# Gated attention with routed experts on one core: token grouping in fewer steps, GpSimd takes mixes, masks and row numbers, four row buffers

## What is computed

```python
xn = _layernorm(x, axis=-1)
s = _L0_attn_ref(xn, ...)          # softmax(q k^T / 4) v, combined with lambda, layernorm, @ Wo + bo
h = jnp.mod(x_flat[:, :2].sum(axis=1).astype(jnp.int32), 8)      # x_flat = xn
sel = jnp.stack([h, jnp.mod(h + 1, 8)], axis=1)
w = jnp.any(sel == e, axis=1) / 2
y = jnp.maximum(x_flat @ W1e + b1e, 0.0) @ W2e + b2e             # for each expert e, acc + w * y
x = x + s * _silu(acc)
```

## Time and profile before

| | us |
|---|---|
| median of 3 runs | 412.05 |
| lowest, highest | 411.11, 412.3 |
| the profiled execution, its own time | 411.52 |
| its span in the profile | 409.6 |
| TensorE busy | 381.5 (93%) |
| VectorE busy | 291.8 (71%) |
| ScalarE busy | 267.5 (65%) |
| GpSimd busy | 189.3 (46%) |

### The profile page before, as it was taken

One profiled execution on the slowest core, in us unless ns is written; L12 is line 12 of the kernel. 1 busy time (PEld: TensorE's weight loads), 2 busy tenths in 40 slices (PEclk: granted clock), 3 DMA queues, 4 the chain that ended last, 5 costly groups with the idle time before them and its releaser, 6 DMA issues.

```text
span 409.6 us, 8427 instructions
## 1 busy us (share of the span) xinstructions
PE 381.5 (93%) x2576; PEld 248.3 (61%) x2576; DVE 291.8 (71%) x758; ACT 267.5 (65%) x667; POOL 189.3 (46%) x262
## 2 busy tenths in 40 slices
PE   4996989999999999999999999999999999999993
PEld 2353876565775667766665668765676667764321
DVE  7787996656686757766676767866686767866884
ACT  3581756666765776576666767676766668675783
POOL 7944203454456543565355532663573444541200
PEclk9996999999999999999999999999999999999999
DMA  7975953263216451265105640346136141216740
GB/s 263 343 230 112 242 196 91 80 206 105 79 37 191 111 195 21 79 190 168 46 27 170 189 140 18 136 121 197 48 127 216 22 169 47 81 26 213 230 159 26
DMA packets 36945, 54.75 MB, mean 134 GB/s; under 512 B 6724, under 2 KB 25141, under 8 KB 36903
## 3 DMA queue, kind: packets, MB, share of 16 engines
q1 hardware_dynamic: 31456, 46.94, 34.6%
q0 software_dynamic: 3296, 6.76, 7.8%
q10 hardware_dynamic: 2151, 0.53, 0.6%
HBM read 15.59 MB, written 6.75 MB: 55 GB/s over the span
## 4 chain that ended last, share of the span: by engine, by line
PE 74%; DVE 7%; DMA 5%; ACT 4%; SPq 4%; issue 4%; POOL 1%; ACTq 0%; DVEq 0%; POOLq 0%
PE ring L1393 14%; PE pv_bank L1327 13%; PE ring L1414 12%; PE score L1289 12%; PE exp L1314 10%; PE ring L1251 3%; DVE neg_max L1049 3%; DMA xs<-xn_rows,inverse 3%; SPq L532 2%; PE ring L1335 2%; PE ring L1255 1%; PE ring L1353 1%; PE ring L1276 1%; PE ring L1375 1%; PE score L1264 1%
## 5 line engine op out<-in xcount | busy, mean ns | idle before, releaser
L1049 DVE TENSOR_REDUCE neg_max<-score 128x1 f32<-128x512 f32 x256 | 169.0, 683 | 72.3 <-PE score L1289 66.7
L1289 PE MATMUL score<-ks,qs 96*128 96x512 bf16 x256 | 98.3, 386 | 6.3 <-DVE neg_max L1049 6.0
L787 ACT ACTIVATE probs<-exp 128x512 f32<-128x512 f32 x124 | 72.5, 605 | 36.3 <-PE exp L1314 32.3
L787 ACT ACTIVATE xin<-exp 128x512 f32<-128x512 f32 x120 | 69.7, 604 | 38.5 <-PE exp L1314 38.1
L1314 PE MATMUL exp<-qs,ks 99*128 99x512 bf16 x244 | 91.7, 380 | 0.1
L825 ACT ACTIVATE hT<-ring,pair 128x128 f32<-128x128 f32 x256 | 73.4, 377 | 13.0 <-PE ring L1393 11.9
L1414 PEld LDWEIGHTS ring<-w_sb,hT 128*128 128x128 f32 x568 | 73.5, 191 | 10.4 <-issue 3.5
L1414 PE MATMUL ring<-w_sb,hT 128*128 (+1 forms) x568 | 75.4, 275 | 0.9 <-ACT hT L825 0.9
L1393 PEld LDWEIGHTS ring<-xsT,pair 128*128 128x128 f32 x512 | 66.3, 191 | 14.6 <-issue 8.1
L1393 PE MATMUL ring<-xsT,pair 128*128 128x128 f32 x512 | 68.2, 276 | 1.7 <-issue 1.2
L684 POOL TENSOR_SCALAR tanh<-tanh 128x128 f32<-128x128 f32 x32 | 17.2, 536 | 95.5 <-ACT tanh L845 95.2
(11 more groups left out here) (198 smaller groups left out, 417.4 us busy)
## 6 DMA issues: line engine op xcount, KB each, us to landing
pair<-table SPq DMA_DIRECT2D x32, 580.0 KB
qs<-parts SPq DMA_DIRECT2D x42, 128.0 KB
ks<-parts SPq DMA_DIRECT2D x42, 128.0 KB
xin<-_attn_hidden_states_dram SPq DMA_DIRECT2D x8, 256.0 KB, 4.4
table<-in_L_ffn_W_dram SPq DMA_DIRECT2D x2, 1024.0 KB, 9.2
w_sb<-in_L_ffn_W_dram SPq DMA_DIRECT2D x8, 256.0 KB, 10.4
xn_rows<-xn SPq DMA_DIRECT2D x8, 256.0 KB, 3.0
table<-_attn_hidden_states_dram SPq DMA_DIRECT2D x8, 256.0 KB, 5.4
```

What stands on the lines that cost most here:

```text
L787: a.activation(prob(n), exp_banks[n][:, :], ACT.Exp, scale=SCALE).then_inc(exp_done, 1)
L1049: v.tensor_reduce(neg_max[:, b % 2, col:col + 1], score_bank[n % 2][:, :], AX.X, ALU.max, negate=True).then_inc(max_taken, 1)
L1289: t.matmul(score_bank[n % 2][:, :], qs[0:MAX_ROW, b % STK, hh, c * P:(c + 1) * P], ks[0:MAX_ROW, b % STK, hh, :], start=True, stop=True).t ...
```

## The change

Grouping: `count_groups` works on the integers without casting them back, adds the mean's part ahead of the wait for `rstd`, and the scan over the one-hots starts one column early, so that it counts the tokens before each one and nothing is subtracted behind it. The second product of `find_tokens` goes to ScalarE. `xn` of batches 4 to 7 is made from the mean and `rstd` in place of `shift`. GpSimd takes from VectorE the masks of the extras, the mix of an extra's row with the one before ("mix_z", in two steps, through `z_mix`), the row numbers and masks of `groups` 2 and 3, and the scaling of `wo_eff` and `lnb_wide`. `XS` is 4. In the table the corrections of the lower parts of batch 1 move from before the inverting matmuls to between the first scores, the loads of initial rows and the extras' steps shift, and the extras follow each other at 2.2 in place of 2.3.

```diff
-PEEL_AT = (((-55.5, -55.3), (-55.4, -55.25)), ((-45.5, -45.3), (-45.4, -45.2)))
+PEEL_AT = (((-55.5, -55.3), (-55.4, -55.25)), ((-45.5, 4.5), (-45.4, 5.1)))
...
-EXTRA_PACE = 2.3
+EXTRA_PACE = 2.2
...
-XS = 3
+XS = 4
@@ schedule: an extra
         at(t + DX - 1, "bias_z", f)
+        if f >= 1:
+            at(t + MIX_AT, "mix_z", f)
@@ names
-        onehot = work[:, 512:768].rearrange("p (e t) -> p e t", e=EXP)
-        seen = work[:, 768:1024].rearrange("p (e t) -> p e t", e=EXP)
+        onehot = work[:, 511:767].rearrange("p (e t) -> p e t", e=EXP)
+        seen = work[:, 767:1023].rearrange("p (e t) -> p e t", e=EXP)
@@ GpSimd
+                elif kind == "extras":
+                    pool.wait_ge(group_x_ready, 1)
+                    g.tensor_tensor(same_tile[:, 1:NX], edge_tile[:, 1:NX], edge_tile[:, 0:NX - 1], ALU.subtract)
...
+                elif kind == "mix_z":
+                    f = s[1]
+                    pool.wait_ge(z_ready, f)
+                    link(g.tensor_scalar(z_mix[:, :], z[:, f - 1, :], same_tile[:, f:f + 1], None, ALU.mult))
+                    pool.wait_ge(z_biased, f + 1)
+                    g.tensor_tensor(z[:, f, :], z_mix[:, :], z[:, f, :], ALU.add).then_inc(z_mixed, 1)
+                elif kind == "groups" and s[1] == 2:
+                    pool.wait_ge(texp_ready, 1)
+                    link(g.tensor_tensor(above, group[:, 1, :], group[:, 0, :], ALU.subtract))
...
+                    g.tensor_copy(init_row[:, :], z_row).then_inc(init_row_ready, 1)
+                elif kind == "fold":
+                    pool.wait_ge(small_loaded, 16 * SMALL)
+                    g.tensor_scalar(wo_eff[:, :], wo_sb[:, :], lnw_sb[:, 0:1], OUT_SCALE * GATE_SCALE, ALU.mult, ALU.mult)
...
@@ ScalarE
+                elif kind == "tokens":
+                    act.wait_ge(in_tile_ready, 1)
+                    a.activation(token[:, 1, :, :, :], in_tile, ACT.Copy, scale=row_of[:, 0:1]).then_inc(token_ready, 1)
@@ VectorE, count_groups
+                dve.wait_ge(rstd_ready, len(LN_GROUPS))
                 link(v.tensor_tensor(v01[:, :], v01[:, :], rstd[:, :], ALU.mult))
-                dve.wait_ge(shift_ready, len(LN_GROUPS))
-                link(v.scalar_tensor_tensor(v01[:, :], shift[:, :], 2.0, v01[:, :], ALU.mult, ALU.add))
...
-                link(v.tensor_copy(n_abs[:, :], whole_i))
...
-                link(v.tensor_copy(whole_i, h[:, :]))
...
-                link(v.tensor_copy(h[:, :], whole_i))
...
-                v.tensor_tensor(seen[:, :, :], seen[:, :, :], onehot[:, :, :], ALU.subtract).then_inc(seen_ready, 1)
+                v.tensor_tensor_scan(work[:, 768:1024], work[:, 511:767], zeros,
+                                     0.0, ALU.add, ALU.add).then_inc(seen_ready, 1)
@@ VectorE, down of an extra
                     if f >= 1:
-                        dve.wait_ge(z_ready, f)
-                        link(v.scalar_tensor_tensor(z[:, f, :], z[:, f - 1, :], same_tile[:, f:f + 1],
-                                                    z[:, f, :], ALU.mult, ALU.add))
+                        dve.wait_ge(z_mixed, f)
```

More of the change, by code:

```diff
@@ L68 @@
 ONES_AT = -45.09
-FFN_FIRST = 7.6
-EXTRA_PACE = 2.3
-STATIC_FIRST = 27.33
-FFN_PACE = 6.85
-TX, DX = 2.4, 3.2
+FFN_FIRST = 7.74
+EXTRA_PACE = 2.2
+STATIC_FIRST = 27.19
+FFN_PACE = 6.86
+MIX_AT = 1.8
+TX, DX = 2.7, 2.7
 PAIR_AT = (20, 21, 22)
-INIT_AHEAD = 1.5
-H1, D0, D1 = 1.8, 3.3, 4.5
+INIT_AHEAD = 2
+H1, D0, D1 = 1.8, 3.3, 4.4
 TT = 2
@@ L627, in _ @@
                     pool.wait_ge(stats_ready, end)
-                    if end < B:
+                    if first not in POOL_NORM:
                         g.tensor_scalar(shift[:, tok], mv[:, tok, 0], -1.0, None, ALU.mult)
@@ L637, in _ @@
                     b = s[1]
-                    pool.wait_ge(shift_ready, 1 + [b >= end for _, end in LN_GROUPS].index(False))
+                    pool.wait_ge(rstd_ready, 1 + [b >= end for _, end in LN_GROUPS].index(False))
                     for t in range(C * b, C * b + C):
-                        last = g.tensor_scalar(xn[:, t, :], xin[:, t, :], rstd[:, t:t + 1], shift[:, t:t + 1],
-                                               ALU.mult, ALU.add)
+                        last = g.tensor_scalar(xn[:, t, :], xin[:, t, :], mv[:, t, 0:1], rstd[:, t:t + 1],
+                                               ALU.subtract, ALU.mult)
                     last.then_inc(xn_ready[b], 1)
@@ L860, in _ @@
             v.memset(zeros, 0.0)
+            v.memset(work[:, 767:768], 0.0)
             link(v.memset(va[:, :, :, :, HD:VW], 0.0))
@@ L1014, in _ @@
                         continue
[L1015 to L1017 removed]
+                    link(v.tensor_tensor(v01[:, :], xin[:, :, 0], xin[:, :, 1], ALU.add))
                     dve.wait_ge(stats_ready, end)
[L1019 to L1020 removed]
+                    v.scalar_tensor_tensor(v01[:, :], mv[:, :, 0], -2.0, v01[:, :],
+                                           ALU.mult, ALU.add).then_inc(pair_summed, 1)
                 elif kind == "transpose_x" and s[1] not in PEELED:
@@ L1171, in _ @@
                     tile = f - NX
+                    if tile == 0:
+                        dve.wait_ge(init_row_ready, 1)
                     dve.wait_ge(y_init[tile % YB], 16 * (tile // YB + 1))
```

90 lines of the change are left out of this document (45 added, 45 removed).

## The result

| | before | changed |
|---|---|---|
| median of 4 runs each, taken together | 411.58 | 417.09 |
| lowest, highest | 409.64, 412.3 | 415.21, 418.07 |
| profiled execution, its span | 411.52, 409.6 | 417.1, 415.3 |
| GpSimd busy | 189.3 | 207.5 |

The ratio is 1.0136, 95% interval 1.0085 to 1.0187: slower by 5.6 us, where 1.85 us of gain were forecast, and outside the range.

What follows compares the result with a forecast made beforehand. TensorE's matmuls were taken to set the pace from 76 to 376 us, leaving time to win where it idles or slows before and at the ends. -1.25 + 0.2 - 0.8 = -1.85 us, giving 410.2 us, range 407.9 to 413.0.

Steps and rivals of the forecast that it cites:

- the first gather is issued, and lands, 0.8 us sooner: End of the grouping: inverse matmuls end sooner, so the first gather of tokens lands at 35.5 us, 0.8 sooner.
- Grouping: Stretch up to the inverse: inverse's matmuls end near 29.8 instead of 30.6 us, ScalarE's token product taking 1.3 us.
- ScalarE's queue, +0.55: Before the first tile: a correction between ScalarE's small loads and the first xsT copy makes that copy 0.55 us later.
- The clock, part of -1.25: Gap before the first tile: corrections there keep TensorE at 2.4 GHz; first down at 40.5, -1.25 us with gather and queue.
- rival (c): From 34 us, before the first tile: clock falls all the same, +1.55 us in all, 413.6 us; chance 0.10.
- The extras' stage, +0.2: 41.75 to 57.95 us: GpSimd's queue gives back 0.2 of the 1.25 us; exp 0 at 56.9.
- rival (b): Extras' stage: GpSimd's queue takes all back, exp 0 at 57.95; -0.5 us, 411.5 us; chance 0.20.
- The wait for the initial rows, -0.8: Behind the extras, near 68 us: earlier last extra and unqueued store nearly remove TensorE's wait for the first tile's initial rows, -0.8 us.
- The steps moved in the rest of the table: 0, bounds -0.3 and +0.3: Behind the first tile: moved steps keep TensorE's count, costed at 0 us, bounds -0.3 and +0.3.
- Rival (d): Mixes in the extras' stage: VectorE and GpSimd hold each other up, about +0.3 us, 412.4 us; chance 0.06.

Runs made afterwards that it cites:

- experiment 1: Changed kernel with GpSimd normalising batches 4 to 7 the old way, (x times rstd) plus shift: 410.87 us, ratio 1.0008 to the kernel before.
- experiment 2: Kernel before with only the new normalising, (x minus mean) times rstd on GpSimd: 415.17 us, ratio 1.0114.
- experiment 12: Changed kernel with the negative mean added in place of the mean subtracted in GpSimd's normalising: 411.12 us, ratio 0.9995 to the kernel before.
- experiment 5: Kernel of experiment 1 with gathers of extras 5 and 6 one mix sooner, the first tile's ahead of the row-number instructions: 411.58 us, ratio 1.001.
- experiment 6: Kernel of experiment 1 with the six mixes back on VectorE as one instruction each: 410.11 us, ratio 1.0005 to the kernel before.
- experiment 7: Kernel before with only the front half: shorter grouping, second token product on ScalarE, moved corrections; old normalising kept: 410.31 us, ratio 0.9977.
- experiment 13: Kernel of experiment 5 with VectorE's find_rows waiting until GpSimd has normalised batch 7: 410.57 us, ratio 1.0004 to the kernel before.
- experiment 4: Kernel of experiment 1 with the corrections of batch 1 back ahead of the inverse: 411.13 us, ratio 1.0012 to the kernel before.
- experiment 8: Kernel of experiment 1 run once more, unchanged, for a second profile: 411.80 us.
- experiment 11: Kernel of experiment 7 with three more matmuls, overwritten later, ahead of the inverse: 411.68 us, ratio 1.0004 to the kernel before.
- experiment 16: Kernel before with only the change's numbers for the static tiles (later order of the table): 409.20 us, ratio 0.9973.
- experiment 15: Kernel of experiment 7 with VectorE's find_rows waiting until GpSimd has normalised batch 7: 409.87 us, ratio 0.9985 to the kernel before.

## Why the prediction was wrong

**The step that failed** is the last line of the grouping, "the first gather is issued, and lands, 0.8 us sooner"; it was issued 6.1 us later and landed 4.0 later. The change replaces (x times `rstd`) plus `shift` by (x minus the mean) times `rstd` in sixteen GpSimd instructions. The grouping step of the sum spoke of what leaves VectorE and costed the gather's time by the row numbers alone. The gather has a second condition, that all of `xn` is stored, and the new form of the normalising, which decides when, was put at nothing without a reason. Before, the last store landed at 29.15 us; with the 0.9 us that pass above from the landing (36.66) to the gather's issue (37.55), this condition stood at about 30.05, only 1.4 us ahead of the gather at 31.45. Now the normalising ends 7.0 us later (32.08 against 25.06) and the store lands 7.5 us later; less the 1.4, that is the 6.1 us by which the gather is late. The instructions took about 0.36 us more each, and the one beside `find_rows` another 1.7: 14.9 us instead of 8.2. The row for the old form was even in the earlier trace rows, used only for another rival. Experiments 1, 2 and 12 show it: +4.7 us with this edit alone, nothing measurable left without it.

**Point by point, for the rest:**
- Grouping: the inverse's matmuls ended at 30.4, not 29.8, as `find_rows` ended at 29.86 and not at 29.2. ScalarE's product took 1.33 us (forecast 1.3), and VectorE did wait for the count matmuls. In experiment 1 it is 8.5 us from the end of these to the end of the inverse instead of 9.0: 0.5 us gained of 0.8. Left out was that VectorE and GpSimd stood close: before, the last normalising ended at 25.06 and VectorE's first product started at 25.22.
- ScalarE's queue, +0.55: wrong. The loads start at 26.76 us, while the correction written ahead of them starts at 29.05; they were no bound. The row misread is the copy at 36.97: its bracket names TensorE's transpose, which ended at 36.86. In experiment 1 the copy comes at 36.22, not 37.5.
- The clock, part of -1.25: right where experiment 1's profile shows it (clock 1.00, first `down` at 40.59 against 40.5). It does not hold in every execution: in the changed kernel and in the profiled executions of experiments 5 to 7 the clock fell between about 28.7 and 30.5 us, behind 1.5 to 1.9 us of idle TensorE ahead of the inverse. The corrections moved into the gap behind had filled that very place; rival (c) looked for the fall behind it. Its 2.6 us for a correction at the low clock were right (2.8), but the fall cost less than it had: from the first transpose to the first `down` 6.4 us in the changed kernel against 4.7 in experiment 1, so 1.6 us, not 3.4.
- The extras' stage, +0.2: mis-sized. It gives back 1.8 us in experiment 1 (from -1.16 at the first `down` to +0.60 at "exp 0"). The prediction had waits of 0.4 to 1.2 us for extras 5 and 6 by GpSimd's queue; measured were 0.71 and 1.43 for extras 4 and 5. By experiments 5 and 6 the queue can be the cause for extra 5 only. Extra 4's gather, issued at 38.97 us, was waited for until 45.1, 6.1 us, where 3.5 to 4.9 were taken; the loads of `w_sb` are under way from 37.5 us, but that they delay it is not shown. The kernel before issued it no sooner (38.76) and wanted it only at 46.12; that the closer order of the extras asks for it too soon is a likely reading, and no run has the change with the old spacing. GpSimd was busy 12.2 of the stage's 16.2 us, not all of it. In time and in "exp 0" this is close to rival (b), whose cause holds for extra 5 alone. Mixes at 1.1 us and small ones at 0.2 to 0.3 were right.
- The wait for the initial rows, -0.8: did not come. In experiment 1 the last extra's row is ready at 59.2 us instead of 60.2, but its store goes out at 61.44 instead of 61.53: it still stands behind a load of weights in SyncE's queue (until 61.40), where the forecast had it free. It lands 0.65 us slower, and the gather goes out at 65.82 us against 65.26.
- "The steps moved in the rest of the table: 0, bounds -0.3 and +0.3": mis-sized. Alone they are worth -1.1 us (-1.8 to -0.4). In the whole change without the new normalising, at +0.3, neither this gain nor that of the front is left; that the extras' stage uses them up is inferred from the 1.8 us above, not shown.
- Rival (d), the two engines in each other's way, had the mechanism, but in the wrong place: in the extras' stage only 0.6 us of waiting for sums is seen, at the grouping a single instruction of 2.56 us. The Trainium skill (SBUF — State Buffer, "SBUF: two separate sides") says that one of the two waits for the whole of the other's instruction. The trace agrees that they hold each other up, and shows that one such wait was not the whole of it: in experiment 5 GpSimd's instruction of 25.96 us was not through when VectorE's product ended (26.63), nor when the first of `find_rows` did (27.50), and ended only at 28.52.

**Still open:** why experiment 13's kernel still reaches 413.3 us (the landing times of the store and of the extras' gathers, which differ by 2 to 3 us between profiles, are candidates), and how much of the front's gain is lost by chance in the long stretch and how much by a rule; profiled executions are too few to tell.

## What to carry to other kernels

When an edit changes the form of an instruction and not only its place, price the new form, and list every condition of the transfer at the end of its chain, not only the one that comes last today; here a condition that came 1.4 us ahead of the last one moved by 7.5. An engine that is made faster next to GpSimd work should be looked at for what it will then run beside. And a reordering that looks incidental can be the best part of a change: try it alone. Two single profiles can differ by more than the edit between them. So before a difference is put down to the edit, take out of it what a landing time or the start accounts for.

## What the runs showed of the hardware

- On GpSimd, 128x128 in f32 with two scalars per partition: 0.45 us with an addition, 0.80 with a subtraction. With one scalar and no second operation 0.60; with a second operation by a constant 0.37, so the fuller form is the cheaper.
- One GpSimd instruction of 0.45 us took 2.56 beside VectorE's back-to-back instructions with two SBUF inputs, and VectorE's products of 128x1248 took 0.94 us there instead of 0.81.
- Row gathers landed 2.8 us after their issue in the median over the kernel of experiment 1 (2.4 to 6.1). The first of all took 4.0 to 5.9 us where it went out by 32.3 us (the kernel before, experiments 1, 4, 6, 8, 11 and 16), 4.9 at 33.09 (experiment 15), and 2.8 to 3.5 where it went out from 33.6 us on. Extra 4's, issued beside the six loads of `w_sb`, was waited for until 6.0 to 6.7 us after its issue in six profiles (experiments 1, 5, 6, 8, 12, 13), but landed after 4.8 and 3.9 us in those of experiments 4 and 16.
- The store of the last normalised rows landed 2.3 to 3.7 us after its issue in the profiles that issued it by 26.9 us, and 4.2 to 5.0 us after it in those that issued it from 27.2 us on. So a late normalising costs more than its own lateness; the cause is open.
